# One LayerNorm step moved from ScalarE to VectorE, and feed-forward work spread thinner between attention steps

## What is computed

```
q, k = elu(x Wq^T)+1, elu(x Wk^T)+1 ;  v = x Wv^T        # 16 heads of 64
kv_sum, k_sum = running sums over the sequence of k v^T and k   # causal
a  = (q . kv_sum) / (q . k_sum + 1e-8)  @ Wo^T
x1 = layernorm(x + a)
h  = layernorm(x1) * gamma + beta
y  = silu(h @ dequant(fc1) + b1) ;  z = y @ dequant(fc2) + b2
out = layernorm(x1 + 0.5 * z)
```

## Time and profile before

| what | us |
|---|---|
| median of three runs | 3196.31 |
| profiled execution | 3198.54 |
| span of the slowest core in it (core 1) | 3197.0 |
| spans of all cores | 3178.5 to 3197.0 |
| PE busy | 2099.3 (66%) |
| DVE busy | 1242.1 (39%) |
| ACT busy | 883.6 (28%) |

### The profile page before, as it was taken

One profiled execution on the slowest core, in us unless ns is written; L12 is line 12 of the kernel. 1 busy time (PEld: TensorE's weight loads), 2 busy tenths in 40 slices (PEclk: granted clock), 3 DMA queues, 4 the chain that ended last, 5 costly groups with the idle time before them and its releaser, 6 DMA issues.

```text
span 3197.0 us, 31221 instructions; the slowest of 8 cores (3178.5 to 3197.0 us)
## 1 busy us (share of the span) xinstructions
PE 2099.3 (66%) x11268; PEld 959.0 (30%) x11268; DVE 1242.1 (39%) x1724; ACT 883.6 (28%) x1172; POOL 64.7 (2%) x126
## 2 busy tenths in 40 slices
PE   1777775556775667576766766677557664776385
PEld 0333332333332333232323322333223322333132
DVE  0555554444315431533244334433423342225314
ACT  0222222234213421342124222422251215122311
POOL 1000000000000000000000000000000000000000
PEclk9888887777797779778887888788879886988598
DMA  9677773000143014311322221322133203310242
GB/s 194 165 215 216 217 217 101 7 7 7 42 109 94 7 32 115 97 34 35 78 75 61 58 58 63 73 56 60 59 77 83 56 1 96 96 53 4 79 119 66
DMA packets 171884, 262.17 MB, mean 82 GB/s; under 512 B 40659, under 2 KB 114387, under 8 KB 169684
## 3 DMA queue, kind: packets, MB, share of 16 engines
q1 hardware_dynamic: 154164, 201.38, 22.5%
q0 software_dynamic: 17568, 58.79, 8.4%
HBM read 251.82 MB, written 33.55 MB: 89 GB/s over the span
## 4 chain that ended last, share of the span: by engine, by line
PE 48%; DVE 18%; DMA 12%; ACT 12%; issue 7%; another core or an unknown queue 2%; SPq 1%; DVEq 0%; ACTq 0%
PE PS L514 14%; PE PS L532 13%; PE PS L327 7%; DMA w1d<-wsl_a 5%; DMA w2d<-wsl_c 5%; PE PS L793 4%; DVE z_sb L543 3%; PE PS L690 3%; ACT h_fm L472 2%; DMA out<-out_s 2%; DVE st_m L765 2%; PE PS L760 2%; DVE r_s L552 1%; DVE u_s L548 1%
## 5 line engine op out<-in xcount | busy, mean ns | idle before, releaser
L532 PE MATMUL PS<-w2r_a,y_fm 128*128 128x512 bf16 x1024 | 285.2, 429 | 221.9 <-DVE z_sb L543 113.1
L327 PE MATMUL PS<-wqkv,x_fma 128*128 128x512 bf16 x1536 | 378.5, 405 | 21.7 <-DVE ksr_f L381 5.8
L520 ACT ACTIVATE y_fm<-PS,b_s 128x512 bf16<-128x512 f32 x256 | 175.9, 687 | 475.8 <-PE PS L514 456.9
L543 DVE TENSOR_TENSOR z_sb<-PS,z_sb 128x1024 f32<-128x1024 f32 x96 | 117.5, 1224 | 479.6 <-PE PS L532 454.7
L514 PE MATMUL PS<-h_fm,w1r_a 128*128 128x512 bf16 x1024 | 259.5, 415 | 63.7 <-ACT y_fm L520 33.6
L514 PE MATMUL PS<-h_fm,w1r_b 128*128 128x512 bf16 x1024 | 247.7, 403 | 23.1 <-ACT t L339 8.9
L532 PE MATMUL PS<-w2r_b,y_fm 128*128 128x512 bf16 x1024 | 254.3, 393 | 0.0
L327 PEld LDWEIGHTS PS<-wqkv,x_fma 128*128 128x128 bf16 x1536 | 155.7, 102 | 242.6 <-issue 85.8
L532 PEld LDWEIGHTS PS<-w2r_a,y_fm 128*128 128x128 bf16 x1024 | 101.0, 106 | 390.9 <-issue 317.5
L514 PEld LDWEIGHTS PS<-h_fm,w1r_a 128*128 128x128 bf16 x1024 | 105.8, 105 | 212.9 <-issue 116.6
L765 DVE TENSOR_TENSOR st_m<-PS,umask 128x1024 bf16<-128x1024 f32 x64 | 78.4, 1224 | 221.0 <-PE PS L760 191.1
(11 more groups left out here) (141 smaller groups left out, 2428.3 us busy)
## 6 DMA issues: line engine op xcount, KB each, us to landing
w2r_a<-w2d SPq DMA_DIRECT2D x32, 1024.0 KB, 5.7
w2r_b<-w2d SPq DMA_DIRECT2D x32, 1024.0 KB, 7.4
out<-out_s SPq DMA_DIRECT2D x32, 512.0 KB, 2.7
s1b_a<-fc1sb SPq DMA_DIRECT2D x4, 2048.0 KB, 10.1
s2b_a<-fc2sb SPq DMA_DIRECT2D x16, 512.0 KB, 8.2
s2b_b<-fc2sb SPq DMA_DIRECT2D x16, 512.0 KB, 4.1
g1a<-fc1q POOLq DMA_DIRECT2D x4, 2048.0 KB, 11.8
g2a<-fc2q POOLq DMA_DIRECT2D x16, 512.0 KB, 5.3
```

Source lines behind the costliest of these rows:

```text
L327: op("tensor", lambda e, d=d, s=s, xfm=xfm: e.matmul(PS[g][:, 512 * s:512 * s + 512], xfm[:, 128 * d:128 * d + 128], wqkv[:, 3072 * d + D ...
L520: op("scalar", lambda e, m=m, lo=lo: e.activation(out=y_fm[:, 512 * (m % 8):512 * (m % 8) + 512], in_=PS0[:, lo:lo + 512], func=AF.Silu, b ...
L532: op("tensor", lambda e, m=m, s=s, rbuf=rbuf: e.matmul(PS0[:, 1024 + 512 * s:1536 + 512 * s], y_fm[:, 512 * (m % 8) + 128 * t: 512 * (m % ...
L543: op("vector", lambda e, t=t: e.tensor_tensor(out=z_sb[:, D * t:D * t + D], in0=PS0[:, 1024:2048], in1=z_sb[:, D * t:D * t + D], op=ALU.ad ...
```

## The change

Two edits. In `layer_norm_tail` the pass at L421 is one VectorE instruction in place of the ScalarE one, with the same operands, output and row sums. In the chunk loop `b3` is (budget + 2) // 3, rounded down, in place of (budget + 1) // 2. Lines below the first edit move down by one.

```diff
-            op("scalar", lambda e: e.activation(out=outap, in_=src, func=AF.Identity,
-                                                bias=s5, scale=s4, accum_out=acc_ap),
+            op("vector", lambda e: e.scalar_tensor_tensor(
+                out=outap, in0=src, scalar=s4, in1=s5.to_broadcast([128, D]),
+                op0=ALU.mult, op1=ALU.add, accum_out=acc_ap),
                 reads=list(src_reads) + [n4, n5], writes=[outname] + acc_w)
...
             budget = (len(B_QUEUE) + rem - 1) // rem if B_QUEUE else 0
-            b3 = (budget + 1) // 2
+            b3 = (budget + 2) // 3
```

## The result

The changed kernel takes 3149.07 us (median of ten runs), the kernel before, run beside it, 3197.77: ratio 0.9858, 95% interval 0.9829 to 0.9888, so 48.7 saved, where the forecast was 3142 against 3196.3, 54.3 saved. The profiled execution took 3143.2 with a span of 3141.6, 55.3 under that of before; it lies at the fast end of its runs, most of which fall between 3144.7 and 3150.6. Ratios, and the times of the experiments, go by the runs in which neither half of the chip (four cores) lags the other by more than 1% at a lower clock, so a ratio need not be the quotient of two medians.

A forecast was written before the change was run, and what follows sets the result against it. The waits between PE's steps, not any engine's busy time, were taken as the bound. 40.0 - 0.3 + 10.1 + 4.0 = 53.8 off 3198.5 gave 3144.7, less 2.2 for the median: 3142; range 3118 to 3160, 0.85 inside.

The forecast's parts named there:

- chunks 12 to 27, order: Four super-blocks each get a PE list that ran elsewhere before and take that list's time: 40.0 gained.
- chunks 28 to 31, order: Last super-block with four closures per slot, added chunk by chunk: 306.9 against 306.6, 0.3 lost.
- ACT free, chunks 4 to 27: ScalarE free 1.71 earlier: 10.1 from Silu stalls behind the LayerNorm tail, 4.0 from copies in slot 5.
- its debt to chunk 31: Chunk 30's last C queues its VectorE pass behind the LayerNorm, so chunk 31's v products wait: 4.3 lost.
- The rival that had the filled chunk 30 bring 26 more: Chunk 30's closures fill its waits: chunks 28 to 30 take 280.1, not 306.9; time 3115; chance 0.13.
- The wait at an F behind the tail: PE's wait for Silu shrinks by 1.69 in chunks 7, 11, 15, 19, 23 and 26: 10.1.
- The rival that the clock would stay up in all six stalls: Shorter gap keeps PE's clock up, 16 matmuls behind it at 3.62 for 5.40: 10.7 more, 3131; chance 0.10.
- The T in slot 5: Its eight ACT copies no longer delay the next chunk's khat: 1.0 each in chunks 5, 9, 13, 17, 4.0.
- The reading that slots hide nothing: Feed-forward closures cost as much in slots as bare: chunk 22's three F and four C 43.3 against 41.9.
- The rival that slots are cover: Slots hide closures, bare stretches lose it: up to 123.7 lost, 3306; slower once over a ninth hidden; chance 0.03.
- VectorE's side: The L421 pass taken at 1.34 on VectorE, L813 within 0.1 of the same time: no cost.
- the last step: From profiled execution to median of runs: 2.2 off 3144.7, giving 3142.5, said as 3142.

The follow-up runs named there:

- the second edit alone: `b3` as in the changed kernel, the pass at L421 still on ScalarE as in the kernel before: 3166.8, ratio 0.9896.
- the run with ACT kept busy: The changed kernel with the old ScalarE pass kept beside the VectorE one, into a tile that nothing reads then: 3166.4, ratio 0.9879.
- one per slot: The changed kernel with never more than one closure per slot (`b3` = min(budget, 1)): 3123.2, ratio 0.9758.
- the first edit alone: The pass at L421 on VectorE, `b3` as in the kernel before: 3185.7, ratio 0.9955.

## Why the prediction was right

By its own steps, forecast and measured, on the slowest cores of the profiled executions and by the median of the eight cores:

| step | forecast | slowest cores | median core | from |
|---|---|---|---|---|
| chunks 12 to 27, order | 40.0 gained | 38.5 | 35.1 | and the second edit alone |
| chunks 28 to 31, order | 0.3 lost | 1.9 gained | 1.1 lost | before and the second edit alone |
| ACT free, chunks 4 to 27 | 14.1 gained | 14.9 | 18.1 | second edit alone to changed kernel, six super-blocks |
| profiled execution (median core: span) | 53.8 | 55.3 | 49.6 | before to changed kernel |

(On the slowest cores the second row is 306.6 to 298.2, and chunk 31 on 254.3 to 260.8, which is 3169.7 - 2908.9. In the third row 4 to 7 went from 304.0 to 299.7, the next five by 3.5, 2.7, 1.0, 1.3 and 2.1. Besides, from the second edit alone to the changed kernel chunk 28 to the end took 1.4 more, and chunk 4 began 1.7 earlier than before; no step has these.)

The mechanism of each step held. That the sum came so near is partly luck: in the kernel before, core 1 took 349.3 in 24 to 27 and 306.6 in 28 to 30, where most cores took 347.2 and 303.2, and the errors of the third row cancel.

The first row is the argument that carried the forecast: a super-block whose list moves can be priced where the list ran before. It held to 0.9 in each.

In the second row the parts were less exact than their sum. Chunk 28 took 114.9 (forecast 112.7), chunk 29 100.8 (101.7), chunk 30 83.6 (88.2), and chunk 31 grew by 6.8 (4.3). Chunk 30 was cheaper and its debt to chunk 31 larger. Part of the debt is the C of the last quarter at its end, whose VectorE passes are paid for a chunk later: 4.29 of waiting for 2.64. The rival that had the filled chunk 30 bring 26 more is wrong; with the second edit alone, filling it bought 8.4 and gave 6.5 back.

In the third row the mechanism was right, and the run with ACT kept busy shows it, but its parts were mis-sized in both directions. The wait at an F behind the tail shrank by 1.69 as written at five of the six places (by 1.06 in chunk 7), but on the slowest cores the matmuls behind it took longer at five, so that the six came to some 6 where 10.1 was forecast. The rival that the clock would stay up in all six stalls came true in none: at 3.62 for 16 matmuls it would have shown, and they took 5.1 to 6.5. The T in slot 5 brought some 7 and not 4.0: chunk 5 went from 43.3 to 41.0, of which 1.1 is the wait for khat; most of the rest is the output product, which took 1.1 less (5.10 to 3.96). And chunk 6, with an F in slots 2 and 4, is faster too (51.1 to 49.9), as are 10, 14 and 18: some 4 in all that the forecast put at nothing.

The reading that slots hide nothing (chunk 22, 43.3 against 41.9) holds as a sum and not by place: an F in slot 2 is hidden on most cores, an F in slot 4 costs 8.9. The rival that slots are cover was to turn the sign once slots hid more than a ninth. They hide about that (an eighth at one per slot), and the sign did not turn, since that ninth left out that two and three per slot cost more than bare: super-block 24 to 27, with L421 on VectorE in both, lasts 344.1 at 3 3 2 1 per slot and 317.0 at 1 1 1 1 (median cores of the first edit alone and of one per slot).

VectorE's side came as forecast, nothing, though the pass itself takes 1.285 (mean of 32) and not 1.225.

The median of the changed kernel lies 7 above the forecast, its profiled execution 1.5 below. The difference comes in at the last step, which took the median of the runs to lie 2.2 below the profiled execution, as it did before; now it lies 5.9 above. What the profiled execution does show is how cores differ: super-block 16 to 19 lasts 320.4 on cores 0 and 5 and 317.0 on cores 1 and 4, with the same list, and chunk 4 begins between 677.0 and 687.6. The slowest of eight cores collects such stretches. Why they fall on a core in one execution and not in another stays open.

## What to carry to other kernels

Where work is interleaved with a chain by a rule, list what the rule puts where; a stretch whose order moves can be priced at the place where the same order already ran. A slot is cover only if the closure fits the wait there and its engines are idle: here transposes at one per slot were free, and one large matmul group per chunk in front of the longest VectorE wait was free on most cores, while the same group in slot 4 cost 8.9 against 7.07 bare. What the C cost in slots the runs do not separate. Take a pass off an engine where another engine's work is queued behind it, even if the engine is idle most of the time.

## What was not expected of the hardware

A shorter idle gap on PE mostly did not shorten the slow stretch behind it. In chunk 11, on all eight cores, 16 matmuls of 512 columns took 5.68 after 4.77 of waiting and 6.51 after 3.08; after 0.48 they took 3.61. But in chunk 23 they went from 5.94 (second edit alone) to 5.13 on most cores. And the length of the wait does not settle it alone: in the run with one per slot, chunk 23, seven cores took 6.35 behind a wait of 3.43 and core 1 took 3.61. Cores 5 and 1:

```profile
2157.00 6.35 PE L515 MATMUL PS<-h_fm,w1r_a 128*128 128x512 bf16 x16 [3.43 <-ACT y_fm L521]
```

```profile
2161.98 3.61 PE L515 MATMUL PS<-h_fm,w1r_a 128*128 128x512 bf16 x16 [3.43 <-ACT y_fm L521]
```

The same chunk 17, with the same instructions, lasts 42.9 on core 5 and 41.2 on core 1 of one execution, with granted clocks of 0.76 and 0.79:

```profile
1678.00:1720.90 42.90, 27.06 (x175) 14.33 (x176) 20.86 (x32) 21.52 (x36) 0.53 (x1) 0.76 0.05 7
```

```profile
1670.40:1711.60 41.20, 25.38 (x174) 13.90 (x174) 20.84 (x32) 21.45 (x36) 0.53 (x1) 0.79 0.05 7
```

The VectorE pass with one operand repeated from a single column took 1285 ns, 60 more than the pass of the same size behind it. Groups by line of the changed kernel:

```profile
L421 DVE SCALAR_TENSOR_TENSOR x_s<-r_sb,stx 128x1024 bf16<-128x1024 f32 x32 | 41.1, 1285 | 4.0 <-DVE stx L418 0.5
L814 DVE SCALAR_TENSOR_TENSOR u_s<-x_s 128x1024 f32<-128x1024 bf16 x32 | 39.2, 1225 | 3.7 <-DVE x_s L421 0.5
```
